# A one-element fill on GpSimd behind every row gather of a graph network's four main stages

## The reference: what is computed

```
x = x + L0(relu(layernorm(x)))      # three SAGE layers
x = x + L1(relu(layernorm(x)))      # one attention layer
# SAGE layer:   agg = segment_sum(h[src], dst) / deg;  h = leaky_relu(agg @ Wl.T + b + h @ Wr.T)
# attention:    h = x @ W;  e = leaky_relu(a_s[src] + a_d[dst]);  softmax of e over the edges of a node
#               out = segment_sum(h[src] * alpha, dst) + bias
```

## Time and profile before

| | us |
|---|---|
| median of three runs | 2769.43 |
| the profiled execution | 2776.93 |
| its span, on which the trace is laid out | 2775.2 |
| PE busy / DVE busy / ACT busy / POOL busy | 1906.9 / 2011.9 / 1325.6 / 1670.8 |
| gathers of L692 (1202 in stages 1 to 3, 405 in stage 4) | 1607 of some 0.96 each |

### The profile page before, as it was taken

The page is one execution under the profiler, slowest core; times in us unless marked ns, Lnnn a source line. Parts: engine busy times, 40 slices in busy tenths (PEclk is TensorE's granted clock), DMA queues, the critical chain, the costliest instruction groups (busy, mean ns, idle before and its releaser), DMA issues. The chain is left out here.

```text
span 2775.2 us, 47937 instructions
## 1 busy us (share of the span) xinstructions
PE 1906.9 (69%) x11800; PEld 1658.6 (60%) x11800; DVE 2011.9 (72%) x8211; ACT 1325.6 (48%) x3517; POOL 1670.8 (60%) x1956
## 2 busy tenths in 40 slices
PE   0005878787784898989894777777776466666565
PEld 0004767676673787778784666666665455555555
DVE  7986555555553787878784888888886688888888
ACT  4893333333340111111111565665656677777776
POOL 5576666666636666666644666666663566666664
PEclk9999999999997999999997999999997788888988
DMA  6885777777773777878774777777776466666766
GB/s 221 277 297 158 219 214 215 214 219 214 215 211 112 212 217 208 222 210 220 216 212 125 206 214 212 214 213 211 214 214 176 120 171 173 170 174 169 177 167 158
DMA packets 618308, 553.89 MB, mean 200 GB/s; under 512 B 75633, under 2 KB 578647, under 8 KB 618000
## 3 DMA queue, kind: packets, MB, share of 16 engines
q1 hardware_dynamic: 374064, 311.88, 38.8%
q0 software_dynamic: 52672, 109.59, 17.9%
q10 hardware_dynamic: 191296, 129.32, 14.4%
HBM read 343.54 MB, written 207.75 MB: 199 GB/s over the span
## 5 line engine op out<-in xcount | busy, mean ns | idle before, releaser
L692 POOL DMA_INDIRECT rows<-tab,idx x1202 | 1158.2, 964 | 720.4 <-issue 300.4
L692 POOL DMA_INDIRECT rows<-tab_c,idx x405 | 385.3, 951 | 273.4 <-issue 100.2
L798 ACT ACTIVATE sage<-bank,b_col 128x256 f32<-128x256 f32 x392 | 184.5, 471 | 760.5 <-remote 343.2
L934 PE MATMUL bank<-mask,rows 128*128 128x128 f32 (+1 forms) x2352 | 434.5, 323 | 97.7 <-issue 85.7
L934 PEld LDWEIGHTS bank<-mask,rows 128*128 128x128 f32 x2352 | 386.3, 199 | 149.1 <-issue 114.4
L1396 DVE TENSOR_TENSOR sage<-bank,sage 128x256 f32<-128x256 f32 x392 | 163.1, 416 | 352.9 <-remote 266.2
L1376 DVE TENSOR_SCALAR mask<-iota,dcol 128x256 f32<-128x256 f32 (+1 forms) x1215 | 413.5, 369 | 0.3
L959 PE MATMUL bank<-sage,wcat 128*128 128x256 f32 x784 | 250.0, 402 | 96.5 <-issue 88.5
L1041 PE MATMUL bank<-ident,mask 128*128 128x128 f32 x784 | 152.7, 327 | 195.7 <-issue 160.6
L1051 PE MATMUL bank<-rows,sage 128*128 128x131 f32 x1568 | 249.3, 310 | 7.1 <-issue 5.3
L1008 PEld LDWEIGHTS bank<-rows,mask 128*128 128x128 f32 x1568 | 213.4, 198 | 45.6 <-issue 36.6
(11 more groups left out here) (228 smaller groups left out, 3716.2 us busy)
## 6 DMA issues: line engine op xcount, KB each, us to landing
sage<-inv_d SPq DMA_DIRECT2D x392, 128.0 KB
turned<-sage ACTq DMA_DIRECT2D x392, 128.0 KB
tab<-sage ACTq DMA_DIRECT2D x392, 128.0 KB
sage<-turned SPq DMA_DIRECT2D x392, 128.0 KB
tab_c<-sage ACTq DMA_DIRECT2D x196, 132.0 KB
own_w<-tab_c SPq DMA_DIRECT2D x196, 132.0 KB
tab<-sage SPq DMA_DIRECT2D x49, 512.0 KB, 3.5
xin<-tab SPq DMA_DIRECT2D x196, 128.0 KB
```

Source lines behind the costliest of these rows:

```text
L692: eng.indirect_dma_start(out=rows[:, s.win[w], 0:width], out_offset=None, in_=table, in_offset=bass.IndirectOffsetOnAxis(ap=idx[:, s.w + w ...
L798: eng.activation(new_t[:, o.v, :], ps_zz[ph][o.t % len(ps_zz[ph])][:, 0:TILE], ACT.Identity, bias=b_col[:, ph - 1:ph]).then_inc(S["z_a"], 1)
L934: m = eng.matmul(to[:, a:b], rows[:, s.win[w], 0:D], mask[:, s.mw[w], c:c + b - a], start=(w == 1), stop=(w == 2))
```

## The change

A tile of 4 x 405 elements for each partition is added, and behind every gather of L692 GpSimd writes 0.0 into one column of it (128 partitions x 1 element, 4 bytes each). Nobody reads the tile; the fill raises no semaphore and waits for none. Each gather has a column of its own. The 13 early gathers at L669 and those of the prologue get no fill. That makes 1607 fills.

```diff
         xin = sb("xin", [P, RING, 2, D])
+        between = sb("between", [P, (LAYERS + 1) * NWIN])
         mask = sb("mask", [P, MRING, TILE])
...
                                                    ap=idx[:, s.w + w:s.w + w + 1], axis=0)
                                                ).then_inc(row_ld[s.q], 16)
+                        at = (ph - 1) * NWIN + s.w + w
+                        eng.memset(between[:, at:at + 1], 0.0)
                 if ph == LAYERS + 1:
                     eng.wait_ge(S["agg_done"], LAYERS * NG)
```

## The result

| | before | after |
|---|---|---|
| median of 9 runs each, same chip | 2771.64 | 2779.73 |
| lowest and highest | 2767.4, 2776.1 | 2776.16, 2783.1 |
| span of the profiled execution | 2775.2 | 2778.0 |

The ratio is 1.0024, with a 95% interval from 1.0016 to 1.0032: 8 us slower, where 70 were forecast. That is just outside the 0.2% that I had called no change, and far from both large cases, A (2840) and B (about 2600). The changed gathers are at L693, the fill at L698; other lines have moved by three (L934 is L937, L1396 is L1399, L798 is L801, L1008 is L1011, L1051 is L1054).

What follows compares the result with a forecast made beforehand. It took the order of work, with PE's signals late while gathers run, as the bound, not an engine's rate. 60 us for stages 1 to 3 plus 10 for stage 4 made +70: 2840 us, 8 in 10 range 2560 to 2890.

Steps and rivals of the forecast that it cites:

- A: Whole kernel, the forecast itself: the fill's time counts in every round, 2780 to 2890 us; chance 0.44.
- B: Whole kernel: a fill between gathers lets PE's late signals through, POOL's waits shrink, about 2600 us; chance 0.40.
- I take 0.05 us: POOL's cost for one fill behind a gather, chosen between the ends 0.00 and 0.18 us.
- 1202 x 0.05 = 60 us: Stages 1 to 3: the fills' whole cost lies on the path, 60 us.
- the lower end: POOL's cost for one fill: 0.00 us, a fill hidden in the 0.30 us of issue.
- rival C: Whole kernel: the fill disappears in the issue gap, distance stays 1.25 us, time within 0.2%; chance 0.10.
- whatever makes a round of gathers longer moves the release: POOL's rounds: signals come 1.0 to 1.1 us after its last gather, so lengthening delays the next round by as much.
- PE's signals are late while gathers run: Main stages: PE's signals become visible late, in a bunch about 1.0 to 1.1 us after a round's last gather.
- prize: POOL's extra waits, 366 us: all gone gives 2483 us, half gone 2666.
- The lateness depends on gathers being neighbours: PE's signals: named as a condition that would make the forecast wrong; no size given.
- DVE's lock: Fills meeting DVE's mask operations: 24% wait 0.18 us, 50 us over stages 1 to 3, kept for the range only.

Runs made afterwards that it cites:

- e8: The kernel before, unchanged, profiled again on a chip of the quicker kind: 2342.26 us, ratio 1.0002 to the kernel before there.

## Why the prediction was wrong

**The step that failed first** is "I take 0.05 us" for a fill, and with it "1202 x 0.05 = 60 us". The distance from gather to gather moved by 0.001 to 0.004 us in the medians, and by nothing where POOL is the bound. That is the lower end that I had named, 0.00, and rival C's row: "Under C the distance is 1.25 us." I chose the other row, an operation of the prologue that ends 1.19 us before the gather behind it ends. But that gather's own row is 1.04 us long, where those of the main stages have 0.94, and I carried the 1.19 over whole. In the kernel after, a gather ends 0.19 + 0.95 = 1.14 us behind the fill's end, and the fill itself, 0.11 us, begins right where the last gather's row ends: 1.25 us. So the 0.30 us in front of a gather aren't a delay that follows whatever came last; a short operation fits into them. The evidence was in the earlier trace rows: an idle time marked "issue" has no owner, and I should have asked whether it is free, and given C far more than 0.10. The 2779.73 us do lie within the 2560 to 2890 that I gave as the wide range. That is no merit: the range was that wide to hold both A and B, and neither happened.

**The step that failed second** is "whatever makes a round of gathers longer moves the release". It was not tested by the change, since nothing became longer, but by the 128-element fill: 0.12 us more for each gather gave +0.26%, and the pauses shrank from 1.3 to 0.9 us. The release that looked tied to POOL's end wasn't. With the first step mended and this one kept, I would have been right by luck; with a fill that really takes time, wrong by 140 us or more.

**Right** was that PE's signals are late while gathers run, and that this, not an engine's rate, sets the time on this chip. The run without gathers in stage 2 shows it, and the one with 256-element fills shows that most signals can pass in time while gathers run. **Rival B's** prize exists, then (the same program takes 430 us less on chips without lateness), but its means fell: an ordinary operation between neighbours doesn't let signals through. In the kernel after every pair of neighbours is parted by a fill, and the lateness is 4.32 us. At a median distance of 1.37 us in stage 1 it is there, at 1.48 it is gone in the median, with three blocks in four. "The lateness depends on gathers being neighbours", which I had named as a way to be wrong, isn't it either.

**DVE's lock.** The up to 50 us that I kept for it didn't come, but the lock is there. The rule of the Trainium skill (SBUF — State Buffer, Who interferes with whom), that DVE's tensor_scalar in its two-port mode and GpSimd shut each other out for a whole instruction, agrees with the trace of the kernel after. Of the 1607 fills 483 begin while DVE builds a mask (a tensor_scalar at L1379 or L1381); they take 166 ns in the mean and up to 348, and 462 of them end 20 to 45 ns behind the mask operation. The 1124 others, beside any other operation of DVE or none, take 116 ns. That is 30% of the fills, where I had reckoned with 24%, and 50 ns for each of them, where I had 180: 24 us over the run. What the prediction had wrong is who pays: the longer fill, too, disappears in the issue gap. The longest ones show it, in stage 2 (DVE, POOL):

```profile
903.34 0.61 DVE L1379 TENSOR_SCALAR mask<-iota,dcol 128x256 f32<-128x256 f32 x2
903.38 0.33 POOL L698 MEMSET between<- 128x1 f32 x1
903.68 1.75 POOL L693 DMA_INDIRECT rows<-tab,idx  x1
```

The last gather began at 902.43, so the distance is 1.25 us as ever, and the gap is used up whole. But this next gather has 1.75 us in place of 0.95. In stage 2 it is so behind 23 such fills, where the kernel before had 13 gathers of over 1.2 us; the stage took no longer (600.9 us from first to last gather, 601.4 before). A fill that lasts pays: with 256 elements DVE is busy for 2084.1 us, 72 more than before, and 68 of them are in the two mask operations alone. Of the page before, then of the page with 256 elements:

```profile
L1376 DVE TENSOR_SCALAR mask<-iota,dcol 128x256 f32<-128x256 f32 (+1 forms) x1215 | 413.5, 369 | 0.3
...
L1381 DVE TENSOR_SCALAR mask<-iota,dcol 128x256 f32<-128x256 f32 (+1 forms) x1215 | 465.5, 412 | 0.3
```

A gather of stages 1 to 3 takes 1017 ns there in place of 964.

**The 8 us that are left** are clear of the noise in the comparison of the result and are not explained. The fills' 0.003 us x 1607 would be 5 us if all of it lay on the path, but in the two traces, which differ by 2.8 us only, the difference stands in stage 3. The 128-element fill costs the same 7 us with 0.12 us more for each gather, so it isn't the distance. On the quicker chip the ratio is 1.0002, so nothing in the program as such costs them.

**Open** is what in the chip makes the signals late, where between 1.37 and 1.48 us of distance it eases, and whether a pause behind each block would lift it. A fill's length changes with the distance, so these runs don't tell the one from the other either. That it belongs to the chip isn't shown: the two comparisons that met the lateness (perhaps on one and the same chip) came first, those on four other chips later, and none of the chips on record was visited a second time, so a passing state is as possible. One more difference stands in the traces. In the kernel before only 1894 of the 5339 semaphore updates that DVE makes have a record, and 618 of ACT's 2319; in e8 it is 5314 and 2309. With that go the waits on "remote", 237 of POOL's before and none in e8. So it may be that the profiler's recording itself has a part in the lateness; no run here shows the time without it.

No version beats both kernels everywhere: the 256-element fill wins 1.1% where the kernel before takes 2772 us, but its shorter relative with 192 elements already loses 12% where it takes 2342. There before and after, equal to each other, are the best.

## What to carry to other kernels

An engine's idle time is not all alike: a gap that stands before every instruction of a kind and is marked "issue" can take up a short operation for nothing, even on the engine that bounds the kernel (129 ns in a gap of 300 here), so price such an addition by what it leaves of the gap. A pause that begins where a row of gathers ends isn't proof that the gathers' length sets it; lengthen them a little and see whether the pause gives way. Pair the rows of two engines by counting blocks, not by their neighbourhood in time. And when waits have no owner and signals arrive microseconds late, run the untouched kernel on other chips before designing around it: what was learned on one may be a loss of 8 to 12% on the others.

## What the runs showed of the hardware that was not expected

- The same program took 2772 us on one chip and 2341 to 2345 us on four others (three to 15 runs a comparison, one run on one of them). The time that the clock can account for is small: in stage 1 the granted clock is 0.96 and 0.99. The difference is when semaphore updates of PE take effect: DVE starts 4.3 us (stage 1) and 5.8 us (stage 2) after the sum's end in the median, against 0.04 us. Whether it is the chip or a state that passes wasn't tested.
- On the slower chip that lateness was there with gathers 1.25 to 1.37 us apart. Without gathers it is 0.04 us, and with 1.48 us from one to the next it is 0.04 us in the median, but up to 5.7 us in stretches.
- A gather of 128 rows takes 1.25 us from one to the next, of which 0.95 are recorded; an operation of 0.11 us, and even one of 0.33 us (903.38), leaves it at that. A wait for that operation's own semaphore in front of the next gather adds 0.08 us to the median distance and 0.12 to the mean. Fills of 128, 192 and 256 elements bring the distance to 1.37, 1.42 and 1.48 us.
- A one-element fill of GpSimd takes 116 ns, but 166 ns in the mean when it begins during a tensor_scalar of DVE, and then it ends about 30 ns behind DVE's operation. Beside DVE's other operations it isn't lengthened.
